# Selective scan, attention and MLP: where the diagonals of B come from

## The reference

```python
dt = jax.nn.softplus(proj[..., :D_INNER] + dt_bias)       # D_INNER = 512
Bm = proj[..., D_INNER:D_INNER + D_STATE]                 # D_STATE = 64
def step(hst, ins):
    dt_t, B_t, C_t, x_t = ins
    dA = jnp.exp(dt_t[:, :, None] * A)
    hst = hst * dA + (dt_t * x_t)[:, :, None] * B_t[:, None, :]
    y_t = jnp.einsum('bds,bs->bd', hst, C_t)
```

## Time and profile before

| | |
|---|---|
| median of three runs | 3630.17 us (3625.3 to 3631.42) |
| the profiled execution's own time | 3631.45 us |
| its span, first to last instruction | 3629.7 us |
| scan, from the first scan of state 0 to POOL's last product | about 66 to 2808 us |
| all instructions | 59786 |
| DMA | 176.17 MB, queue q1 busy 15.4% of 16 engines |
| granted clock of PE, mean | 0.971 of full |

### The profile page before, as it was taken

One profiled execution on the slowest core, in us unless ns is written; L12 is line 12 of the kernel. 1 busy time (PEld: TensorE's weight loads), 2 busy tenths in 40 slices (PEclk: granted clock), 3 DMA queues, 4 the chain that ended last, 5 costly groups with the idle time before them and its releaser, 6 DMA issues.

```text
span 3629.7 us, 59786 instructions
## 1 busy us (share of the span) xinstructions
PE 3354.8 (92%) x22946; PEld 2574.8 (71%) x22946; DVE 3002.5 (83%) x2916; ACT 3032.8 (84%) x5112; POOL 2568.4 (71%) x1577
## 2 busy tenths in 40 slices
PE   8998999899989999998899899989899989999999
PEld 5888888888878888887888888878788432222244
DVE  4988999899889989988899899889999478888241
ACT  6999999999999999999899999998998336777620
POOL 2989998899999989999998899999789000000000
PEclk8999999999999999999999999999999998999999
DMA  3111111111112111111111111111111043211000
GB/s 101 52 44 47 53 53 55 47 53 47 55 52 75 53 49 52 48 55 47 54 59 49 47 53 53 52 61 53 47 46 44 10 109 66 31 24 18 1 6 18
DMA packets 65213, 176.17 MB, mean 49 GB/s; under 512 B 13697, under 2 KB 17537, under 8 KB 64673
## 3 DMA queue, kind: packets, MB, share of 16 engines
q1 hardware_dynamic: 64930, 172.36, 15.4%
HBM read 162.83 MB, written 9.44 MB: 47 GB/s over the span
## 4 chain that ended last, share of the span: by engine, by line
PE 43%; ACT 29%; POOL 20%; DVE 6%; issue 2%; DMA 0%; SPq 0%; DVEq 0%; POOLq 0%; ACTq 0%
POOL arena L649 18%; PE psum L1223 14%; ACT arena L883 12%; ACT arena L869 11%; PE psum L1440 8%; PE psum L1435 6%; PE psum L1432 4%; PE psum L1527 3%; PE psum L1516 3%; PE psum L1491 2%; DVE arena L1129 2%; DVE row_max L1176 2%; POOL carry L645 1%; PE psum L1460 1%; POOL arena L630 1%
## 5 line engine op out<-in xcount | busy, mean ns | idle before, releaser
L649 POOL TENSOR_TENSOR arena<-arena 128x1024 f32<-128x1024 f32 x1024 | 2425.0, 2384 | 158.8 <-DVE arena L1129 115.9
L883 ACT ACTIVATE arena<-arena,a_neg 128x512 f32<-128x512 f32 x2048 | 1459.3, 713 | 0.3
L1129 DVE TENSOR_TENSOR_SCAN arena<-arena,psum 128x512 f32<-128x512 f32 x1024 | 1175.7, 1204 | 166.2 <-PE psum L1435 101.5
L1440 PE MATMUL psum<-ident,arena 128*128 128x128 f32 x8192 | 1255.0, 277 | 38.4 <-POOL arena L649 38.2
L1129 DVE TENSOR_TENSOR_SCAN arena<-arena,carry,psum 128x512 f32<-128x512 f32 x1024 | 1220.2, 1260 | 83.0 <-ACT arena L883 45.3
L869 ACT ACTIVATE arena<-arena,bT 128x512 f32<-128x512 f32 x1536 | 1093.8, 712 | 0.0
L1435 PE MATMUL psum<-ident,arena 128*128 128x128 f32 x6144 | 1023.5, 276 | 0.0
L1440 PEld LDWEIGHTS psum<-ident,arena 128*128 128x128 f32 x8192 | 969.4, 142 | 67.1 <-POOL arena L649 63.8
L1432 PE MATMUL psum<-arena 128*128 128x128 f32 x4096 | 831.2, 285 | 133.1 <-DVE arena L1129 91.2
L1432 PEld LDWEIGHTS psum<-arena 128*128 128x128 f32 x4096 | 658.0, 194 | 359.1 <-issue 131.7
L1435 PEld LDWEIGHTS psum<-ident,arena 128*128 128x128 f32 x6144 | 756.3, 144 | 0.0
(11 more groups left out here) (118 smaller groups left out, 1272.0 us busy)
## 6 DMA issues: line engine op xcount, KB each, us to landing
arena<-bc_dram SPq DMA_DIRECT2D x256, 512.0 KB, 3.6
arena<-qk_dram SPq DMA_DIRECT2D x96, 128.0 KB
qk_dram<-arena SPq DMA_DIRECT2D x12, 512.0 KB, 4.9
arena<-in_x SPq DMA_DIRECT2D x4, 512.0 KB, 10.9
arena<-in_up_w SPq DMA_DIRECT2D x1, 2048.0 KB, 12.0
out_xT<-arena SPq DMA_DIRECT2D x8, 256.0 KB, 2.2
arena<-in_mlp_w SPq DMA_DIRECT2D x3, 512.0 KB, 6.3
arena<-in_fwd_xproj_w SPq DMA_DIRECT2D x1, 1280.0 KB, 10.2
```

Of the source, the lines that this page charges most:

```text
L649: pool.tensor_tensor(h_now[:, f:f + NI // 2], h_now[:, f:f + NI // 2], c_row, ALU.mult)\
L883: act.activation(decay[:, w % 2, f], dt_[:, u % 2, f], ACT.Exp, scale=a_neg[:, d, f, st:st + 1])\
L1129: dve.tensor_tensor_scan(hs[:, w % RING, f, way], decay[:, w % 2, f, way], psum[:, 4 + n % U_BANKS, way], carry[:, st, f:f + 1] if hi else ...
L1440: return pe.matmul(psum[:, c, f * P:(f + 1) * P], hs[:, w % RING, f, c * P:(c + 1) * P], ident[:, :], is_transpose=True, start=False, stop ...
```

## The change

The diagonals of B of units 1 to 7 are no longer made by ACT. A DRAM buffer `diag_dram` holds, for two units in turn, a 128x128 matrix for each of the 64 states. In unit 0 SP fills both halves with zeros, from a zero tile in SBUF, one fill of 256 KB behind each load of C. At pairs 19 to 26 of a unit SP writes the first 128 columns of the next unit's rows of B onto the diagonals, in eight DMAs of eight states (stride 129 elements). Behind each load of C it then loads the two diagonals of the pair after the next, 128 KB, into a ring of three pairs. `turn_u` waits for that load in place of an ACT instruction. Unit 0 still has its diagonals from ACT, written to the same ring. `uT` shrinks to the three blocks left, and ring and zeros lie in the room that this frees. DVE's copy of the rows also waits for the stores of the unit before.

```diff
+DIAG_PAIRS = 3
+FILLS = 16
+DIAG_STORES = 8
...
-        uT = cut(R_UT, 2, TB, DI)
+        uT = cut(R_UT, 2, TB - DIAGS, DI)
+        diag = cut(R_UT + 2 * (TB - DIAGS) * DI, DIAG_PAIRS, 2, P)
+        zeros = cut(R_UT + 2 * (TB - DIAGS) * DI + DIAG_PAIRS * 2 * P, 2 * P)
...
+        diag_dram = nc.dram_tensor("diag_dram", [2, DS, P * P], F32).ap()
...
+            def fill_diag(k):
+
+                half, part = divmod(k, FILLS)
+                if k == 0:
+                    sp.wait_ge(s["zeros_set"], 1)
+                n = DS // FILLS
+                dst = diag_dram[1 - half, part * n:(part + 1) * n].rearrange("n (k t) -> (n k) t", t=2 * P)\
+                    .rearrange("(p r) t -> p r t", p=P)
+                sp.dma_start(dst, zeros.unsqueeze(1).to_broadcast([P, n // 2, 2 * P]))                    .then_inc(s[f"diag_zero_{1 - half}"], 16)
+
+            def store_diag(u, part):
+
+                if part == 0:
+                    sp.wait_ge(s["bc_rows_ready"], u + 1)
+                if u < 3 and part == 0:
+                    sp.wait_ge(s[f"diag_zero_{u % 2}"], 16 * FILLS)
+                n = DS // DIAG_STORES
+                rows = slice(part * n, (part + 1) * n)
+                sp.dma_start(diag_dram[u % 2, rows, ::P + 1], bc_rows[rows, 0:P], allow_slow_non_contiguous=True).then_inc(s["diag_out"], 16)
+
+            def load_diag(p):
+
+                u, pair = divmod(p, DS // 2)
+                if u == 0 or u == UNITS:
+                    return
+                if pair == 0:
+                    sp.wait_ge(s["diag_out"], 16 * DIAG_STORES * u)
+                sp.wait_ge(s["u_full"], NI * 2 * (p - DIAG_PAIRS + 1))
+                n = p - DS // 2
+                if n >= 2:
+                    sp.wait_ge(s[f"diag_in_{p % 2}"], 16 * (n // 2))
+                src = diag_dram[u % 2, pair * 2:pair * 2 + 2].rearrange("n (k t) -> k n t", t=P)
+                sp.dma_start(diag[:, p % DIAG_PAIRS], src).then_inc(s[f"diag_in_{p % 2}"], 16)
+
...
                     if pair == BC_STORE_PAIR and u < UNITS - 1:
                         store_c(u + 1)
+                    if u == 0:
+                        fill_diag(pair)
+                    if 0 <= pair - BC_STORE_PAIR - 1 < DIAG_STORES and u < UNITS - 1:
+                        store_diag(u + 1, pair - BC_STORE_PAIR - 1)
+                    load_diag(p + 2)
...
+            pool.memset(zeros, 0.0).then_inc(s["zeros_set"], 1)
...
                 if w >= 2:
                     act.wait_ge(s["u_full"], NI * (w - 1))
-                src = ident[:, :] if c < DIAGS else dtxT[:, u % 2, c]
-                act.activation(uT[:, w % 2, c, 0:P if c < DIAGS else DI], src, ACT.Copy,
-                               scale=bT[:, u % 2, c, st:st + 1]).then_inc(s["uT_ready"], 1)
+                if c >= DIAGS:
+                    act.activation(uT[:, w % 2, c - DIAGS], dtxT[:, u % 2, c], ACT.Copy, scale=bT[:, u % 2, c, st:st + 1])\
+                       .then_inc(s["uT_ready"], 1)
+                elif u == 0:
+                    act.activation(diag[:, w // 2 % DIAG_PAIRS, w % 2], ident[:, :], ACT.Copy, scale=bT[:, 0, c, st:st + 1])\
+                       .then_inc(s["uT_ready"], 1)
...
                     dve.wait_ge(s["bc_out"], 16 * u)
+                    dve.wait_ge(s["diag_out"], 16 * DIAG_STORES * (u - 1))
...
                 n = NI * w + f
+                p = w // 2
                 if f == 0:
-                    pe.wait_ge(s["uT_ready"], TB * (w + 1))
+                    pe.wait_ge(s["uT_ready"], TB * (w + 1) - max(0, w + 1 - DS))
+                if f == 0 and w % 2 == 0 and w >= DS:
+                    pe.wait_ge(s[f"diag_in_{p % 2}"], 16 * ((p - DS // 2) // 2 + 1))
...
                         o = pe.matmul(dst[:, c * P:(c + 1) * P], dtxT[:, w // DS % 2, c, f * P:(f + 1) * P],
-                                      uT[:, w % 2, c, 0:P], start=True, stop=True)
+                                      diag[:, p % DIAG_PAIRS, w % 2], start=True, stop=True)
                     else:
-                        o = pe.transpose(dst[:, c * P:(c + 1) * P], uT[:, w % 2, c, f * P:(f + 1) * P], ident[:, :])
+                        o = pe.transpose(dst[:, c * P:(c + 1) * P], uT[:, w % 2, c - DIAGS, f * P:(f + 1) * P], ident[:, :])
```

More of the change, by code:

```diff
@@ L189, in build @@
             s2_full probs_ready pv_done attn_copied sums_full sums_copied recip_ready attn_ready v_ready
-            c_in_0 c_in_1""".split()
+            c_in_0 c_in_1 zeros_set diag_zero_0 diag_zero_1 diag_out diag_in_0 diag_in_1""".split()
         s = {n: sem(n) for n in names}
```

## The result

The changed kernel takes 3614.7 us (median of six, 3613.34 to 3616.99), the kernel before in the same comparison 3629.97 us (3625.3 to 3631.42): 0.9961 of it, 95% interval 0.9948 to 0.9973. That is 15.3 us faster where 23 to 24 was forecast, inside the range. The profiled execution took 3613.34 us with a span of 3611.6 us; against the profiled one before it is 18.1 us shorter.

The account below looks back on a forecast made before the run. No engine alone was taken to bound the kernel; ACT binds the scan only in parts. Odd units 10.5, even 7.5 and unit 7 6.2 us sum to 24.2 saved, added work 0: 3607 us, range 3587 to 3634.

Parts of the forecast that it names:

- The removal: ACT's 448 diagonals in units 1 to 7 go: 178 us of busy time, 24.2 us of it saved in the kernel.
- ceiling of 47 us: Most the removal could gain: 161 states on ACT's chain in units 1 to 7, at 0.29 us each.
- The added work: New memset on POOL, fills, stores and loads of diagonals on SP: all hidden, 0 us, with a store taken at 5 us.
- rival (c): Slow stores delay loads of C in units 0 to 6: 59 us, 3666 at 10 us each; slower cases together 0.13.
- The odd units: Scan windows of units 1, 3 and 5, read from unit 3: 3.5 us saved a unit, 10.5 together.
- the start of a unit: First eight states of an odd unit: 4.2 states on ACT's chain, 1.2 us saved, POOL leaving room of 2.8.
- window of 37.5 us: Last eight states of unit 3, DVE, ACT and POOL full together at 4.69 us a state: nothing saved.
- The even units: Units 2, 4 and 6, where POOL also saves the carry: 1.8, 2.8 and 2.9 us saved, together 7.5.
- rival (a): Give-back: savings end at the next engine, only diagonals inside the two bursts per unit count: 6 us, 3625; chance 0.21.
- window of 40.3 us: Eight states of an even unit, POOL busy 39.02 us at its floor: expected to keep its time.
- Unit 7: The last unit's scan, where ACT binds in parts: 1.0, 3.2 and, in its first sixteen states, 2.0 us; together 6.2.

Follow-up runs that it names:

- e3: Kernel before, with each ACT diagonal of units 1 to 7 made twice, 448 more activations: 3682.2 us, 1.0143.
- e1: Changed kernel without its new DMAs and the waits on them, PE multiplying by the identity in units 1 to 7: 3618.4 us, 0.9966 of the kernel before.
- e2: Kernel before, ACT's diagonals kept, with all the new DMAs added and no wait of PE on them: 3628.9 us, 0.9998.
- e6: Kernel before with the softplus burst cut, Abs and Exp going block by block behind each copy of dt: 3617.1 us, 0.9958.
- e9: Changed kernel with each store of diagonals issued four times: 3619.1 us, 0.9970 of the kernel before.
- e4: Changed kernel with each of the 56 stores of diagonals issued eight times: 3819.2 us, 1.0523 of the kernel before.
- e5: Changed kernel with the softplus burst cut, Abs and Exp going block by block behind each copy of dt: 3601.3 us, 0.9917 of the kernel before.

## Why the prediction was right, and where its terms were off

**The removal.** Right in kind: 448 instructions went, ACT's wait for PE took their place with the same releaser and grew (148 to 225 us). The ceiling of 47 us was not tested as a ceiling; as a price for the same work added it came close (e3: 52 us). The busy time saved was 116 us and the waits grew to 225, where I had said 178 and 300.

**The added work.** Right: e1 and e2 give it nothing that can be told, on both sides. The store was assumed at 5 us; alone it is through about 3 us after its issue, and in a row each takes 1.8 to 2.0 us. The Trainium skill's rules on transfers under 512 bytes and on strided last dimensions (DMA: Bandwidth & Descriptors, Specifications and Rules for kernel authors) do not decide here. With the second the trace agrees: 1047 packets under 512 bytes for 1024 elements. Whether each is also read and written back no run here shows. By those rules rival (c) would have gained; the measurement decides against it.

**The odd units: the term that failed.** I gave the start of a unit 1.2 us, because ACT held 4.2 states of the chain there and POOL's busy time left 2.8 us of the window. Half of that room was the lowered clock of unit 3's start: in unit 1, at full clock, POOL is as busy and the window is 44.0 us. Unit 1 had the same clock before and after, and shows 44.0 us both times: nothing gained. Before (the whole first window and the states 4 to 7 in it), then after:

```profile
421.80:465.80 44.00, 40.38 (x343) 38.13 (x344) 40.48 (x37) 38.13 (x67) 42.53 (x22) 1.00 0.15 51
447.10:465.80 18.70, 17.51 (x155) 16.77 (x153) 18.70 (x17) 18.70 (x34) 18.63 (x9) 1.00 0.17 58
```

```profile
420.70:464.70 44.00, 41.62 (x349) 38.94 (x349) 40.52 (x38) 37.10 (x62) 42.21 (x22) 1.00 0.20 65
445.90:464.70 18.80, 18.79 (x161) 17.58 (x159) 18.80 (x18) 18.80 (x32) 18.44 (x9) 1.00 0.23 72
```

Of the 44 us, some 25 are the turn of the unit, where everybody waits; in the states behind it DVE is as full as ACT, 18.70 of 18.70. After the change PE, DVE and ACT are all full there, and a state still takes 4.7 us, as in the window of 37.5 us where DVE was full both times. A full ACT alone would not prove that ACT sets the pace: it is full in both rows, with its diagonals and without. Room must be read over the states in which the engine holds the chain, not over the window: the idle time that I took for room lay elsewhere in it. The chain names one of several engines that end together. This failed step is worth 1.2 us in four units, 4.8 us.

The other odd terms by undisturbed windows: steps 8 to 15 -0.8 (forecast 0.8); 16 to 23 none (none); 24 to 31 -0.7 (1.0); 40 to 47 -0.3 (0.5); and -0.3 in 32 to 39, which I had at nothing. Together 2.1 us a unit for 3.5.

**The even units.** At full clock the first window fell from 41.9 us (unit 2 before) to 40.8 (unit 6 now), and 0.6 us of it came back in the next, which rose from 40.9 to 41.5 (unit 2 before, then unit 6 of the changed kernel):

```profile
755.50:797.40 41.90, 38.70 (x333) 36.80 (x332) 38.69 (x37) 37.76 (x67) 39.65 (x31) 1.00 0.15 52
```

```profile
2102.40:2143.20 40.80, 38.60 (x334) 36.84 (x333) 38.44 (x38) 34.68 (x58) 37.96 (x30) 1.00 0.21 66
2143.20:2184.70 41.50, 40.05 (x307) 34.52 (x305) 37.92 (x35) 36.91 (x61) 40.22 (x33) 1.00 0.21 64
```

That is rival (a), give-back, at work on a part of the gain. The window of 40.3 us that I expected to stay takes 40.8 in units 4 and 6 now; in unit 2, with its full clock at the start, it took 40.7 before already. With 0.4, 0.3 and 0.3 us in the windows from step 24 on, an even unit gains about 1.5 us, for 1.8 to 2.9 forecast.

**Unit 7.** -0.8, -1.3 and -1.1 us in steps 8 to 15, 32 to 39 and 40 to 47: 3.2, for 6.2. The start (1.2) and steps 24 to 31 (1.0) gave nothing.

Summed, 3 x 2.1 + 3 x 1.5 + 3.2 = 14 us, close to the 15.3 of the medians, and about half of it lies in the windows at and between the two bursts of units 1 to 6. The result lies halfway between the 6 us of rival (a) and the forecast's 24. Of the other 4.1 us between the two profiled executions, 2 lie in units 1 to 7, where the granted clock makes the windows differ both ways, 0.5 in unit 0, and the rest ahead of the scan and behind it. In the kernel before, PE's clock is lowered for a few microseconds at the start of units 3 to 7, in the changed one only of 2 and 4; with it an odd start takes 45.2 to 45.7 us, without it 44.0, with ACT's diagonals and without (e6, with them, has both kinds; e1, without them, has both kinds too). This comes and goes between executions, 1.3 to 2 us at a time, and is probably a part of why e1 and e9 scatter to 3618 and 3619 (the start of the scan moves too, from 65.9 us in the changed kernel to 67.7 in e1); the profiles of single executions can't prove that for the medians.

## What to carry to other kernels

Where several engines are within a few per cent of each other, as here, the share of an engine in the chain tells what it costs to load it further, not what it brings to relieve it; for that, find in the very states that it holds how full the next engine is. ACT works ahead through two buffers here, and still most of what was cut from its softplus burst came off the time, with its diagonals and without; cutting the burst was worth as much (15 us) as taking out 448 instructions elsewhere. And when a trace blames a wait on a DMA, see whether another release falls in the same instant before building on it.

## What the hardware showed that I had not expected

A DMA that writes 1024 separate pieces of 4 bytes to DRAM held SP for 1.8 to 2.0 us when such DMAs followed each other, 1.7 to 1.9 ns a piece, and for 0.33 us when it came alone. With eight in a row the 16 DMA engines were, in the mean, mostly at a fifth of their time (the slices of the window of e4 from 656 to 674 us), while the pieces of a lone store passed within a microsecond. Both point to a limit on the way from SP's issue to the engines; how the pieces are spread over the engines these views don't show, and no run tests it apart:

```profile
DMA  4222222222798999532222222222222222222422
```

A copy of two columns lasts 0.2 us on POOL and 0.4 us (397 ns) on DVE between scans, where it delays the next scan by 0.29 us from its start.

PE's granted clock was 0.90 or 0.93 over the windows of steps 40 to 47 of units 1 to 6, before and after the change, in which it stood for 6 to 7 us behind ACT's softplus burst (unit 3); of its two levels (1.2 and 2.4 GHz) it had the lower one for part of the window. With the burst cut by some 2.5 us PE stood for 4.3 us (unit 5 of e5), and the clock was 0.96 over that window in units 3 and 5 of e5 and 0.93 in the others, so the cut did not take the lowered clock away. At the start of a unit PE stood for 2.0 to 2.1 us in every one of units 1 to 7, before and after; the lower clock followed in five of the seven before and in two of them after.
